# A decoder's second layer with its two batches half a group apart

## The reference

```python
x = _layernorm(x + _L1_attn_ref(x, L1_attn_W_qkv, L1_attn_W_out), axis=-1)
x = _layernorm(x + _L1_xattn_ref(x, ctx_1024, ctx_1024, mask_Bx1x1xS2_ff1, ...), axis=-1)
x = _layernorm(x + _L1_ffn_ref(x, L1_ffn_w_gate, L1_ffn_w_up, L1_ffn_w_down), axis=-1)
...
def _L1_xattn_ref(query, key, value, mask, wq, bq, wk, bk, wv, bv, wo, bo):   # 16 heads of 16
    q = query @ wq + bq
    k = key @ wk + bk
    v = value @ wv + bv
...
    score = jnp.einsum('bhqd,bhkd->bhqk', q, k) / jnp.sqrt(jnp.float32(HD))
    score = score + (1.0 - mask) * -1000000000.0
    alpha = jax.nn.softmax(score, axis=-1)
    context = jnp.einsum('bhqk,bhkd->bhqd', alpha, v)
...
    return context @ wo + bo
...
def _L1_ffn_ref(x, w_gate, w_up, w_down):                                     # hidden width 704
    gate = fp4_linear(x, w_gate)      # both operands quantised to FP4 in blocks of 16
    y = fp4_linear(x, w_up)
    h = jax.nn.silu(gate) * y
    return fp4_linear(h, w_down)
```

## Time and profile before

| | us |
|---|---|
| median of 3 runs (3174.97 to 3189.74) | 3188.46 |
| the profiled execution | 3187.25 |
| its span, first to last instruction | 3185.5 |
| granted TensorE clock over the span | 0.73 |
| second layer's loop, from the first L2185 (2631.8) | 553.7 |
| one loop body (one group of both batches) | 136.4 |

### The profile page before, as it was taken

How to read it: one execution, slowest core, us unless ns; L and a number is a source line. 1 busy time by engine, 2 the same in 40 slices (tenths; PEclk the granted TensorE clock), 3 DMA queues, 4 the chain that set the end, 5 groups by cost and what they waited for, 6 DMA issues and landing times. The chain is left out here.

```text
span 3185.5 us, 41817 instructions
## 1 busy us (share of the span) xinstructions
PE 2136.5 (67%) x11068; PEld 1196.0 (38%) x11068; DVE 2168.2 (68%) x10065; ACT 1752.2 (55%) x5691; POOL 654.1 (21%) x343
## 2 busy tenths in 40 slices
PE   5333644556464555546558999999999927777686
PEld 2222433434343333434443333333333314445353
DVE  4899999989999998999724555555555462534535
ACT  2578888888888888888623444444444411121121
POOL 0000000000000000000013666666666700000000
PEclk8655565565666556565668999999999957877787
DMA  3622222222222222222000000000000021011000
GB/s 94 143 53 58 49 59 48 64 47 54 57 49 59 48 63 47 64 48 64 19 4 4 12 16 15 13 12 15 15 13 12 11 68 62 7 33 40 0 7 7
DMA packets 86782, 123.30 MB, mean 39 GB/s; under 512 B 17445, under 2 KB 65225, under 8 KB 86601
## 3 DMA queue, kind: packets, MB, share of 16 engines
q1 hardware_dynamic: 86600, 121.37, 16.0%
HBM read 100.33 MB, written 21.00 MB: 38 GB/s over the span
## 5 line engine op out<-in xcount | busy, mean ns | idle before, releaser
L1417 ACT ACTIVATE mix_cand<-mix_pre,mixer_cbuf 128x32 f32<-128x32 f32 x2048 | 593.0, 290 | 185.2 <-DVE mix_pre L1352 100.9
L1414 ACT ACTIVATE mix_cand<-mix_state,mixer_cbuf 128x32 f32<-128x32 f32 x2048 | 652.6, 319 | 31.5 <-DVE mix_state L1344 3.1
L1339 DVE SCALAR_TENSOR_TENSOR mix_prod<-mixer_keys,mixer_cbuf,mix_cand 128x65 f32<-128x65 f32 x2048 | 581.4, 284 | 53.2 <-ACT mix_cand L1417 47.0
L1844 DVE TENSOR_REDUCE self_tops<-self_rough 128x2 f32<-128x1024 f32 x256 | 311.6, 1217 | 411.5 <-PE self_rough L1616 411.5
L1352 DVE SCALAR_TENSOR_TENSOR mix_pre<-mixer_keys,mix_gap,mix_state 128x32 f32<-128x32 f32 x2048 | 525.4, 257 | 28.0
L1344 DVE SCALAR_TENSOR_TENSOR mix_state<-mix_cand,mixer_cbuf 128x32 f32<-128x32 f32 x2048 | 506.3, 247 | 0.0
L1830 POOL TENSOR_TENSOR self_psum<-self_psum,self_prob 128x1024 f32<-128x1024 f32 x192 | 451.2, 2350 | 160.6 <-ACT self_prob L1757 151.2
L1446 PE MATMUL mix_out<-all_ident,mix_state 128*128 128x128 f32 x512 | 160.6, 413 | 448.0 <-ACT mix_flat L1400 394.5
L1757 ACT ACTIVATE self_prob<-self_sco 128x1024 f32<-128x1024 f32 x256 | 261.5, 1024 | 118.8 <-PE self_sco L1629 104.8
L1453 PE MATMUL mix_out<-mixer_qbd,mix_flat 128*128 128x4 f32 x1024 | 208.4, 335 | 144.7 <-ACT mix_flat L1400 144.7
L858 POOL TENSOR_TENSOR mix_st_norm_rstd<-mix_st_norm_var,mix_half 128x2 f32<-128x2 f32 x24 | 16.7, 697 | 1370.9 <-DVE mix_st_norm_var L851 1370.9
(11 more groups left out here) (392 smaller groups left out, 3313.1 us busy)
## 6 DMA issues: line engine op xcount, KB each, us to landing
mixer_keys<-k_rows SPq DMA_DIRECT2D x256, 260.0 KB, 4.9
aT_rows<-self_aT SPq DMA_DIRECT2D x32, 256.0 KB, 2.3
two_aT<-aT_rows SPq DMA_DIRECT2D x8, 1024.0 KB, 8.3
coef_rows<-mixer_coef SPq DMA_DIRECT2D x4, 1280.0 KB, 6.6
mixer_cbuf<-coef_rows SPq DMA_DIRECT2D x64, 80.0 KB, 5.5
k_rows<-mixer_krow SPq DMA_DIRECT2D x32, 65.0 KB, 3.9
proj_xin<-in_xT SPq DMA_DIRECT2D x8, 256.0 KB, 4.7
mix_st_xin<-in_x SPq DMA_DIRECT2D x8, 256.0 KB, 5.6
```

Of the source, the lines that this page charges most:

```text
L1339: dve.scalar_tensor_tensor(prod[:, b, :], keys[:, h, b, s_, :], coef(NIB, h, s_, b), cand[:, b, s % 2, :], ALU.mult, ALU.mult, accum_out=g ...
L1414: act.activation(cand[:, b, (s + 1) % 2, NS:2 * NS], state[:, hp, sp_, b, :], ACT.Copy, scale=cbuf[:, h, KEEP, b, s_:s_ + 1]).then_inc(kep ...
L1417: act.activation(cand[:, b, (s + 1) % 2, 0:NS], pre[b], ACT.Tanh, scale=cbuf[:, h, BETA, b, s_:s_ + 1]).then_inc(c_ready[b], 1)
L1844: dve.tensor_reduce(tops[:, kh, t, :], rough[:, :, :], AX.X, ALU.max).then_inc(rough_taken, 1)
```

## The change

The chains are taken half a group apart, and the loops are written out. A *phase* holds the front half of one chain's group (projection, norm 1, cross attention) beside the back half of the other's (norm 2, feed forward, norm 3). There are nine: the first has only a front half, the last only a back half.

What sets the order within a phase is now a table, `PhaseTimes`: for each engine two rows of nominal times in us, one for the segments of the front half and one for those of the back half. `in_time` always takes the segment with the smaller time. SyncE's loads and stores alternate by chain.

```diff
+def in_time(*parts):
+    parts = [(iter(times), part) for times, part in parts]
+    due = []
+    for n, (times, part) in enumerate(parts):
+        next(part)
+        due.append((next(times), n))
+    while due:
+        at, n = min(due)
+        due.remove((at, n))
+        times, part = parts[n]
+        if next(part, parts) is not parts:
+            due.append((next(times), n))
...
+    PE = (0, 8.5, 13, 17, 20, 25, 26.5, 33, 39, 47), (8, 10.5, 18, 26, 28, 36, 38, 40)
+    DVE = ((-1, -1, 7, 8, 8.8, 9.1, 10.4, 19, 22, 24.4, 43, 46.5),
...
-            with sp.Fori(0, NG - 1, 1) as g:
-                for c in chains:
-
-                    wait_apart(sp, (w_loaded, 16), c.norm1.ready, g + 1)
-                    load(g + 1, c)
-                store(g)
-            store(NG - 1)
+            one, two = chains
+            load_next(1, one)
+            for g in range(NG):
+                load_next(g + 1, two)
+                store(g, one)
+                load_next(g + 2, one)
+                store(g, two)
...
+        def phases():
+
+            one, two = chains
+            yield (one, 0), None
+            for g in range(NG):
+                yield (two, g), (one, g)
+                yield (one, g + 1) if g + 1 < NG else None, (two, g)
...
-            with pe.Fori(0, NG, 1) as g:
-                in_turns(*(c.pe(pe, g) for c in chains))
+            for x, f in phases():
+                in_time(*([(PhaseTimes.PE[0], x[0].pe(pe, x[1]))] if x else []), *([(PhaseTimes.PE[1], f[0].ff.pe(pe, f[1]))] if f else []))
...
-            with dve.Fori(0, NG, 1) as g:
-                in_turns(*(c.dve(dve, g) for c in chains))
+            for x, f in phases():
+                in_time(*([(PhaseTimes.DVE[0], x[0].dve(dve, x[1]))] if x else []), *([(PhaseTimes.DVE[1], f[0].ff_dve(dve, f[1]))] if f else []))
```

More of the change, by code:

```diff
@@ L2188, in pe @@
                 yield from self.xa.pe(pe, g, self.xT, self.flip1.ready)
-                yield from self.ff.pe(pe, g)
             def act(self, act, g):
-                for part in (self.flip1, self.xa, self.ff):
+                for part in (self.flip1, self.xa):
                     yield from part.act(act, g)
             def pool(self, pool, g):
-                for part in (self.norm1, self.norm2, self.norm3):
-                    yield from part.pool(pool, g)
+                yield from self.norm1.pool(pool, g)
             def dve(self, dve, g):
@@ L2203, in dve, with ff_pool, ff_dve @@
                 yield from self.xa.dve(dve, g)
+            def ff_pool(self, pool, g):
+                for part in (self.norm2, self.norm3):
+                    yield from part.pool(pool, g)
+            def ff_dve(self, dve, g):
                 yield from self.norm2.dve(dve, g)
@@ L2219, in _, with store, load_next @@
                 load(0, c)
-            def store(g):
-                for c in chains:
-                    wait_apart(sp, (w_loaded, 16), c.norm3.ready, g + 1)
-                    sp.dma_start(out[c.ch.b, bass.ts(g, GT), :].rearrange("(j p) c -> p j c", p=P), c.x[:, :, :]).then_inc(c.stored, 16)
-            with sp.Fori(0, NG - 1, 1) as g:
-                for c in chains:
-                    wait_apart(sp, (w_loaded, 16), c.norm1.ready, g + 1)
-                    load(g + 1, c)
-                store(g)
-            store(NG - 1)
+            def store(g, c):
+                sp.wait_ge(c.norm3.ready, g + 1)
+                sp.dma_start(out[c.ch.b, bass.ts(g, GT), :].rearrange("(j p) c -> p j c", p=P), c.x[:, :, :]).then_inc(c.stored, 16)
+            def load_next(g, c):
+                if g < NG:
+                    sp.wait_ge(c.norm1.ready, g)
+                    load(g, c)
+            one, two = chains
[5 more added lines that the diff above has]
+                store(g, two)
             for c in chains:
                 sp.wait_ge(c.stored, 16 * (NG + 1))
+        def phases():
[4 more added lines that the diff above has]
+                yield (one, g + 1) if g + 1 < NG else None, (two, g)
         @block.tensor
@@ L2238, in _ @@
             pe.wait_ge(w_loaded, 16)
[L2239 to L2240 removed]
+            for x, f in phases():
+                in_time(*([(PhaseTimes.PE[0], x[0].pe(pe, x[1]))] if x else []), *([(PhaseTimes.PE[1], f[0].ff.pe(pe, f[1]))] if f else []))
         @block.scalar
         def _(act):
[L2244 to L2245 removed]
+            for x, f in phases():
+                in_time(*([(PhaseTimes.ACT[0], x[0].act(act, x[1]))] if x else []), *([(PhaseTimes.ACT[1], f[0].ff.act(act, f[1]))] if f else []))
         @block.gpsimd
         def _(pool):
[L2249 to L2250 removed]
+            for x, f in phases():
+                in_time(*([(PhaseTimes.POOL[0], x[0].pool(pool, x[1]))] if x else []), *([(PhaseTimes.POOL[1], f[0].ff_pool(pool, f[1]))] if f else []))
         @block.vector
```

5 lines of the change are left out of this document (added).

## The result

The changed kernel takes **3270.8 us** (median of 4 executions, 3267.9 to 3275.1) against 3188.4 before: a ratio of 1.027, 95% interval 1.024 to 1.030. It is 82 us slower; the prediction said 53, and 3268 was the end of its range.

A forecast was written before the change was run, and what follows sets the result against it. TensorE and its waits were taken to bound the kernel: a phase 40.8 + 22.4 + 8.0 = 71.2 us; 56 + 7 x 71.2 + 52.5 = 606.9 against 553.7, so 3188.5 + 53, rounded to 3241 us, range 3195 to 3268.

The forecast's parts named there:

- The clock term: TensorE time lost to half clock behind three long waits and in the rough passes: 8.0 us a phase.
- half clock nearly throughout: Rival: windows at 1.2 GHz stretch into each other; clock 12 us, a phase 75.2, total 3269 us; chance 10%.
- The seven waits: All TensorE waits in a full phase, 22.4 us in sum, against 17.0 in half a body before.
- Quantised x: TensorE's wait for VectorE's norm 2 and quantising, held back by the other batch's store: 6.3 us a phase.
- maxima: TensorE's wait for VectorE's reductions, three quantising steps of the other batch and the copies: 4.4 us a phase.
- Exp: TensorE's second half of the scores waits for ScalarE's Exp to read the banks it overwrites: 4.2 us a phase.
- hidden-row flips: Three short TensorE waits behind ScalarE's Exp and VectorE's last steps, 0.6, 0.5 and 1.9: 3.0 us a phase.
- Table loads: ScalarE's table loads rise from 8 to 15 in all, each priced at 1.28 us.
- Lone phases: First phase, cross attention of one batch alone, 56 us; last phase, feed forward alone, 52.5 us.
- Work 40.8: TensorE's full-clock work for one batch of one group: cross attention 24.2 and feed forward 16.6, together 40.8 us.
- Queues and loops: SyncE's loads and stores, GpSimd's three small powers per group and the vanishing loops' register steps: no cost or gain.
- If norm 2 is not held by the store: Sign on VectorE: TensorE's wait for quantised x would then fall to 3.1 us and the total by 22 us.

The follow-up runs named there:

- heat_averaging: The changed kernel with six idle f32 products on TensorE between the wait for the last Exp and the averaging: 3261.6 us, ratio 1.024.
- gate_late: The changed kernel with TensorE's second gate and up block moved behind the second rough pass (18 to 21 in the table): 3250.3 us, ratio 1.018.
- no_silu: The changed kernel with ScalarE's Silu replaced by a copy, so that its phases' 14 table loads fall away: 3248.7 us, ratio 1.018.
- half_reordered: The changed kernel, still half a group apart, with other table numbers, so another order on all four engines: 3223.7 us, ratio 1.012.
- written_out: The kernel before with the second layer's loops over the groups written out, order unchanged: 3189.6 us, ratio 1.001.
- half_heat: half_reordered with idle f32 products in four of TensorE's waits: 3181.0 us, ratio 1.000 to the kernel before.
- copies_first: The changed kernel with VectorE's copies of the maxima put ahead of two quantising steps: 3267.0 us, ratio 1.023.
- heat_maxima: The changed kernel with eight idle f32 products ahead of TensorE's wait for the maxima: 3254.0 us, ratio 1.022.
- heat_all: The changed kernel with idle f32 products in five of TensorE's waits: 3240.3 us, ratio 1.017.
- before_heat: The kernel before with idle f32 products in three of TensorE's waits of each batch: 3179.5 us, ratio 0.996.
- store_wait_late: The changed kernel with norm 1's wait for the store moved behind norm 2 and four quantising steps in VectorE's order: 3264.9 us, ratio 1.023.

## Why the prediction was right and wrong

It was right in the sign, in the mechanism of the waits and nearly in both lone phases; its number was 30 us short. One term of the sum was far too small, another too large, and the second hid half of the first.

- *The clock term, 8.0 us a phase: this is the step that failed.* Busy time was to be 40.8 + 8.0 = 48.8 us a phase and was 57.1, 8.3 more, 58 us in seven phases. By the count of busy time at half clock it cost about 15.0, and the work is 42.1, so 7.0 of the 8.3 are the clock and 1.3 are work left out of the 40.8. The prediction had "three waits of over 4 us recur, each followed by some 2.5 us of work lost ... and the rough passes lose 1". Half of the busy time in the stretches shown above is 3.0 us behind the quantised x and 2.4 behind the maxima, which is near the 2.5. It is 3.1 behind the casts, around the rough pass, where I had 1. And behind the wait for Exp it is 8.7 in a phase of 77 us (2.5 and 3.2, 5.7, in one of 73), where I had 2.5. There stand the scores and the averaging, and the loss went on for 20 us. heat_averaging and gate_late, which leave the sum of the waits nearly as it is, show that this depends on what stands behind a wait.
- *My own figures pointed that way,* as I see only now. The kernel before lost 20.7 us a body and had four waits of 4 us or more, two in the earlier trace rows (12.3 and 4.0) and these (9.3 and 4.1):

```profile
PE two_bank L2061 <- DVE two_ff_hq L2008: 11.7, 3, 9.3
PE two_bank L522 <- DVE two_x L499: 4.1, 1, 4.1
```

That is 5.2 us lost for each and not 2.5; three such waits a phase would have made it 15.5. And its averaging ran at full clock, with no wait longer than the 1.8 us for the maxima close ahead of the scores.

- *The rival "half clock nearly throughout"* (10%, a phase 75.2, 3269) came within 2 us in the total and 0.3 in the phase. Its mechanism, windows at half clock that stretch into each other, is what stands behind the wait for Exp (0.50 for 20.5 us on end), so I gave it too little. Its number is luck in part: it had the clock at 12 (measured about 15) and the waits at 22.4 (18.4), and its name says too much, since the clock was 0.72 to 0.79.
- *The seven waits, 22.4 us: measured 18.4.* Quantised x 6.3, measured 5.4 (the store's head-of-line wait is there, with 2.2 us for the 3.2 of the earlier trace rows); norm 1's end 1.3, measured 0.5; casts 1.8, 1.7; second gate block 1.4, 0.7 and 1.4 in turns; maxima 4.4, 4.1; Exp 4.2, 4.0; hidden-row flips 3.0, 1.7: two of the three short waits weren't there. None was too low, and together they hid half of the clock's miss.
- *Table loads at 1.28 and nothing more*: right, by the row (1.28, the next instruction 0.01 behind) and by no_silu (2.4 us of waits a phase for two loads).
- *Lone phases, 56 and 52.5*: measured 58.4 and 53.6.
- *Work 40.8*: about 42 by the count above. The last projection, taken at 3.8 on the reading that gaps of its one-row products don't shrink with the clock, takes 3.4 at full clock (2916.00 to 2919.37), and the one-row products of half a batch 0.62 where they took 1.14 at half clock: the gaps do shrink. Other pieces were too low: the two blocks of gate and up take 9.8 (4.9 each at full clock in half_reordered) for the 9.4, the four pieces of hidden-row transposes some 1.9 (0.48 each, 2975.38 to 2975.86) for the 1.4.
- *Queues and loops at nothing*: the loops are confirmed by written_out; that SyncE's queue costs nothing was only argued.
- *"If norm 2 is not held by the store ... the total falls by 22 us"*: the experiment gave 6 in the median, and single executions lay between 8 us above the changed kernel and 20 below. That the clock makes this difference isn't shown.

What isn't settled: why the clock comes back ahead of the averaging in every second phase only, which makes the 77 and the 73 us, and why phases of the same instructions take 58.7 and 67.9 us in half_heat; and whether more idle products would put the offset below the kernel before.

## What to carry to other kernels

Where waits are short and many, read the granted clock of the work that stands behind each wait before pricing it. Here a wait cost its length and the half clock behind it. In a 77 us phase the 5.4 us wait for the quantised x, ahead of full products, was followed by 6.0 us of busy time at 0.50 (3.0 lost, if half of it is), even the 1.7 us wait for the casts by 6.3 (3.1 lost), and the 4.0 us wait for Exp, ahead of scores and averaging, by 17.4 (8.7 lost). Offsetting two chains by half a group gives each wait one cover instead of its twin and adds a lone phase at either end (36 us here for four groups); try first to let one batch's chain of links finish ahead of the other's within the group. And a wait that is removed from a fixed order can turn up at the next segment, as in two of the four edits here (copies_first, gate_late), so make the sum over all of them.

## What the hardware showed that I had not expected

- Products of 77 rows and 32 columns didn't bring the clock back from 0.50 in 7 us of unbroken work. At the same place, six full products did in 5.1 us, and the averaging behind them ran at 1.00.
- Useless work made the kernel that it was added to faster in five of five runs: 17 and 30 us in heat_maxima and heat_all, 9 in heat_averaging, 43 in half_heat against half_reordered, 9 to 11 in before_heat.
- One program can show two times: store_wait_late took 3251 (twice) and 3279 us (twice). Without a profile of the faster ones the cause is open.
